# Who issues the transposing DMAs of the gathered rows: the sync engine instead of ScalarE

## What is computed

```python
logits = flat_x @ gate_w.T
scores = softmax(logits, axis=-1).T                 # 16 x T
topk_weight, topk_idx = top_k(scores, C)            # each expert takes C = 2 T / 16 = 1024 tokens
xg = flat_x[topk_idx]
g = einsum('ecd,eid->eci', xg, Wg)
u = einsum('ecd,eid->eci', xg, Wu)
h = gelu(g) * u
eo = einsum('eci,edi->ecd', h, Wd) * topk_weight[..., None]
flat_out = zeros.at[topk_idx].add(eo)
shared = gelu(x @ Sg.T) * (x @ Su.T) @ Sd.T         # for all tokens
x = x + layernorm(flat_out + shared)
```

## Time and profile before

| | us |
|---|---|
| median of three runs | 2062.1 (2060.92 to 2062.88) |
| the profiled execution, whole | 2058.04 |
| its span in the trace | 2056.0 |
| PE busy | 1999.6 (97%) |
| PEld busy | 1700.2 (83%) |
| DVE busy | 1360.3 (66%) |
| ACT busy | 1029.1 (50%) |
| POOL busy | 518.5 (25%) |

### The profile page before, as it was taken

How to read it: one execution, slowest core, us unless ns; L and a number is a source line. 1 busy time by engine, 2 the same in 40 slices (tenths; PEclk the granted TensorE clock), 3 DMA queues, 4 the chain that set the end, 5 groups by cost and what they waited for, 6 DMA issues and landing times.

```text
span 2056.0 us, 29853 instructions
## 1 busy us (share of the span) xinstructions
PE 1999.6 (97%) x11050; PEld 1700.2 (83%) x11050; DVE 1360.3 (66%) x2549; ACT 1029.1 (50%) x1900; POOL 518.5 (25%) x604
## 2 busy tenths in 40 slices
PE   7999999999999999999999999999999999998996
PEld 6888888888888888878887888888888888887885
DVE  6676576686666678676767666665656656565648
ACT  4564564574554434454445445454545455454445
POOL 0021021022021000224323332433243323331246
PEclk9999999999999999999999999999999999999998
DMA  3011111111115211234343334443444344435366
GB/s 116 1 42 43 62 63 42 61 62 42 42 55 205 84 62 48 97 96 84 84 98 89 94 81 102 81 111 79 109 86 101 80 108 92 97 86 154 76 216 164
DMA packets 118795, 179.67 MB, mean 87 GB/s; under 512 B 71952, under 2 KB 88464, under 8 KB 111504
## 3 DMA queue, kind: packets, MB, share of 16 engines
q1 hardware_dynamic: 30880, 124.55, 16.7%
q0 software_dynamic: 25392, 37.77, 11.6%
q10 hardware_dynamic: 62400, 15.73, 4.2%
HBM read 102.97 MB, written 59.31 MB: 79 GB/s over the span
## 4 chain that ended last, share of the span: by engine, by line
PE 62%; DVE 3%; ACT 2%; ACTq 2%; POOL 1%; issue 1%; DMA 0%; DVEq 0%; SPq 0%; POOLq 0%
PE mo_psD L1506 9%; PE mo_psG L60 7%; PE mo_psU L60 7%; PE mo_psU L62 7%; PE mo_psU L61 7%; PE mo_psG L62 7%; PE mo_psG L61 7%; PE mo_psD L1508 5%; ACTq L1592 2%; PE mo_psD L60 1%; PE mo_psD L62 1%; PE mo_psD L61 1%; PE mo_psX L1229 1%; ACT mo_halves L1586 1%; ACT mo_HF L1635 0%
## 5 line engine op out<-in xcount | busy, mean ns | idle before, releaser
L1635 ACT ACTIVATE mo_HF<-mo_psG 128x512 f32<-128x512 f32 x320 | 191.7, 599 | 410.7 <-PE mo_psU L62 376.8
L1506 PE MATMUL mo_psD<-wd,mo_H_hi 128*128 128x512 f32 x1024 | 364.6, 396 | 15.6 <-DVE OUT L1922 15.6
L2121 POOL DMA_INDIRECT ACC<-OUT,mo_GI x128 | 204.9, 1601 | 663.2 <-DVE OUT L1922 642.6
L1835 DVE TENSOR_TENSOR mo_HF<-mo_psU,mo_HF 128x512 f32<-128x512 f32 x320 | 220.4, 689 | 222.3 <-ACT mo_HF L1635 218.0
L1508 PE MATMUL mo_psD<-wd,mo_H_lo 128*128 128x256 f32 x1024 | 290.1, 283 | 0.0
L60 PE MATMUL mo_psG<-mo_XT_hi,wg_hi 128*128 128x512 f32 x640 | 256.1, 400 | 2.9 <-DVE mo_HF L1835 2.4
L60 PE MATMUL mo_psU<-mo_XT_hi,wu_hi 128*128 128x512 f32 x640 | 253.5, 396 | 0.0
L62 PE MATMUL mo_psU<-mo_XT_hi,wu_lo 128*128 128x512 f32 x640 | 252.6, 395 | 0.0
L62 PE MATMUL mo_psG<-mo_XT_hi,wg_lo 128*128 128x512 f32 x640 | 252.5, 395 | 0.0
L61 PE MATMUL mo_psU<-mo_XT_lo,wu_hi 128*128 128x512 f32 x640 | 252.4, 394 | 0.0
L61 PE MATMUL mo_psG<-mo_XT_lo,wg_hi 128*128 128x512 f32 x640 | 252.4, 394 | 0.0
(11 more groups left out here) (307 smaller groups left out, 4223.3 us busy)
## 6 DMA issues: line engine op xcount, KB each, us to landing
X1a<-wg_in SPq DMA_DIRECT2D x16, 1024.0 KB, 4.9
X1a<-wu_in SPq DMA_DIRECT2D x16, 1024.0 KB, 4.8
X1a<-wd_in SPq DMA_DIRECT2D x16, 1024.0 KB, 4.8
XN<-XG SPq DMA_DIRECT2D x8, 1088.0 KB, 4.1
X<-x_in SPq DMA_DIRECT2D x8, 1024.0 KB, 6.6
out_dram<-X SPq DMA_DIRECT2D x8, 1024.0 KB, 4.7
XN2T<-xn2T SPq DMA_DIRECT2D x8, 1024.0 KB, 4.0
mo_F<-ACC SPq DMA_DIRECT2D x7, 1024.0 KB, 12.0
```

Source lines behind the costliest of these rows:

```text
L1506: pe.matmul(psD[:, t % 2, :], h_hi, wd_both[:, it, :, :].rearrange("p z d -> p (z d)"), start=(it == 0), stop=False)
L1635: a.activation(HF[:, it % 2, :], psG[:, it % 2, :], ACT.Gelu).then_inc(s_gelu, 1)
L1835: v.tensor_tensor(HF[:, it % 2, :], psU[:, it % 2, :], HF[:, it % 2, :], ALU.mult).then_inc(s_mul, 1)
L2121: g.indirect_dma_start(out=io["ACC"], out_offset=bass.IndirectOffsetOnAxis(ap=GI[n % 2][:, 4 * tb + t:4 * tb + t + 1], axis=0), in_=OUT[:, ...
```

## The change

The function `turn_rows` moves from ScalarE's program to the sync engine's. ScalarE still splits the rows and increments s_half2, but issues no transposing DMA. The sync engine issues them in its loop over the experts: the one of half 1 of expert n between the loads of wg and wu of expert n + 1, the one of half 0 of expert n + 1 behind the load of wu, each behind a wait for s_half2. The first two expert blocks are left out as before.

```diff
@@ scalar
-            def turn_rows(b):
-                wait(a, s_half2, rows_index(b))
-                a.dma_start(out=turned[:, :, :].rearrange("p z (m t) -> p (z m) t", t=P),
-                            in_=halves[:, :, :, :, :].rearrange("p z k t d -> p (z k t d)"), transpose=True).then_inc(s_tt, 16)
-
...
                     if it < 2 and E0 + BY_PE <= b + 1 < D0:
                         split_rows(b + 1, it)
-                        if it == 1:
-                            turn_rows(b + 1)
                     task = weight_task(b, it)
@@ sync
+            def turn_rows(n, tb):
+                if 2 * n + tb >= BY_PE:
+                    wait(sp, s_half2, 2 * n + tb + 1 - BY_PE)
+                    sp.dma_start(out=turned[:, :, :].rearrange("p z (m t) -> p (z m) t", t=P),
+                                 in_=halves[:, :, :, :, :].rearrange("p z k t d -> p (z k t d)"), transpose=True).then_inc(s_tt, 16)
+
             for n in range(E):
                 load_w("d", n)
                 if n < E - 1:
                     load_w("g", n + 1)
+                turn_rows(n, 1)
+                if n < E - 1:
                     load_w("u", n + 1)
+                    turn_rows(n + 1, 0)
                 if 1 <= n < GROUPS - 1:
                     topk.store(sp, n + 1)
```

## The result

The changed kernel is faster: 2043.99 us median (2041.67 to 2045.05, four runs) against 2061.51 of the kernel before, measured on the same chip. The ratio is 0.9914, with a 95% interval of 0.9897 to 0.9931, a gain of 17.5 us. Two further sets of runs, each with its own runs of the kernel before, gave 2038.31 against 2058.1 (ratio 0.9908, interval 0.9893 to 0.9923) and 2043.04 against 2062.49 (0.9904, 0.9889 to 0.9920): gains of 19.8 and 19.5 us. The forecast was 2040.9 (range 2036 to 2052), a gain of 21.2.

A forecast was written before the change was run, and what follows sets the result against it. The prediction took TensorE to bound the kernel, with short waits caused by 30 transposing DMA issues on ScalarE. Terms 1.20 + 7.83 + 3.98 + 8.19 = 21.2 us off 2062.1 gave 2040.9 us, range 2036 to 2052.

The forecast's parts named there:

- The bound and the mechanism: TensorE bounds the kernel; it waits where ScalarE's transposing DMA issue stands before the evacuation of psD; 64.4 us mostly hidden.
- The term of the early blocks: 12 blocks from 899.98 to 1326.25: 7.83 us over 12 clean blocks of 34.87 us, to be removed.
- the term of the later ones: 16 blocks from 1326.25 to 1866.71: 3.98 us over 16 clean blocks of 33.53 us, to be removed.
- the last block's 8.19: Block from 1866.71 to 1908.43: 8.19 us excess from the longest transposing DMA issue and the slow clock behind it.
- Spare time of 0.3 us at the tightest place: Where mo_lo and a weight quarter both precede the evacuation: chain moves up about 1.8 us, a stall costs 1.57.
- The partial rival: VectorE's product and split still hold the evacuation, so only part is gained: 2044 to 2052 us, chance 0.11.
- The sync engine's queue: 30 issues added to an almost idle queue, costed at nothing; cover 19.2 us before the load of wd.
- The landing: Transposed rows reach VectorE's copies (L1750) in time: 4.3 us median, 12.3 at most, against 14.36; price zero.
- the slower rival: Transposing DMAs land too late for VectorE's copies at L1750, deciding from 14.4 us landing on; chance 0.04.
- The 8.18 us: Longest issue, the last transposing DMA on ScalarE's queue, placed where the burst of loads was in flight on the other queue.
- More than I count: More of the same stall in the last block in unprofiled runs: gain up to 25 us, 2034 to 2037, chance 0.08.
- no change: Stalls are displaced, coming from DMA traffic and not from the issue: about 2062 us, chance 0.07.

The follow-up runs named there:

- the second pair of profiles: The changed kernel and the kernel before, both unaltered, each profiled once more: spans 2036.2 and 2057.4 us.
- the complement: Kernel before with 29 transposing DMAs moved to the sync engine, the last one still on ScalarE's queue: 2043.46 against 2062.49 us, ratio 0.9908.

## Why the prediction was right, and where not

**The bound and the mechanism** were right: of 64.4 us of issue time only what reached TensorE counted. The work put back on ScalarE brought the stalls back without a DMA issue there.

**The sum.** 21.2 us was the forecast; the blocks of the changed kernel gave 20.3, the medians 17.5, 19.8 and 19.5. The term of the early blocks, 7.83, was 7.27, since in this profile five of the twelve stay about 0.1 us above the clean block (in the second the twelve are 0.1 over in sum); the term of the later ones, 3.98, was 3.62; the last block's 8.19 was 8.17, and with it the clock. The forecast lies 3.1 us below the first median. Of that 0.9 is this. The rest is of the size of the scatter of the stretch before the first block, which differs by up to 5.4 us between profiles and which I had taken as fixed; that it is this scatter is not shown for the runs without a profile, and the profiled execution, late in that stretch, was the fastest of its four. That the second pair of profiles differs by just 21.2 us is partly luck: the last stall was 0.4 us longer there, which made up for most of what stays.

**Spare time of 0.3 us at the tightest place.** Measured 0.40. The partial rival falls with it: with the issue gone, no evacuation was late.

**The sync engine's queue** cost nothing, as forecast. Issue times there reached 3.60 us at most.

**The landing.** The bound of 12.3 us was the traced maximum, and 14.36 was taken for the limit. It isn't the tightest pair: the kernel before has 13.76 us from issue to reader in every second block, and the changed kernel has the same:

```profile
1350.85 1.97 ACTq L1592 DMA_TRANSPOSE mo_turned<-mo_halves  x1
...
1364.61 1.38 DVE L1750 COPY mo_XTF<-mo_turned 128x1024 uint16<-128x1024 uint16 x2
```

So the slower rival would have begun 0.6 us earlier than the prediction says, at 13.8 us; with landings of 4.3 nothing hung on it. The last DMA on ScalarE's queue behind the burst took 14.4 in one kernel, so the upper bound from one trace was too low; the changed kernel isn't touched by that, since its last DMA goes ahead of the burst.

**The 8.18 us.** The forecast took the whole term as one that goes with the move; it did. Where it put the long issue down to the burst alone, it was incomplete: the same DMA behind the same burst took 2.47 and 1.72 us from another place in the queue. The move of the other 29 would have been enough to be rid of nearly all of it.

**More than I count, no change:** neither. The Trainium skill's remark that another issuer only saves the sequencer's time, usually small (the same page, section "Issuing engines are not separate DMA queues"), holds here in its first half: what was saved is that time and the slow clock behind the longest stall. Its second half doesn't hold so well: the issue takes 1.82 us of a landing of 4.3 (medians). It was worth 0.9% because the evacuations stood behind it in ScalarE's program.

**A sign that I gave and that doesn't hold:** I wrote that the "issue" waits of ScalarE before OUT would be gone. The view of the changed kernel still has them:

```profile
ACT OUT L1691 <- issue: 63.0, 27, 2.3
```

There is no issue on ScalarE any more; these are evacuations between two tiles of TensorE, 2.3 us each, for which no releaser was recorded. The second profile of the same kernel has no such row and puts the time down to TensorE, 128 waits where the first had 101:

```profile
ACT OUT L1691 <- PE mo_psD L1508: 240.5, 128, 2.8
```

The row for wg_hi is gone. "issue" in this view means only that nothing visible was waited for.

## What to carry to other kernels

A DMA issue is an instruction of the engine that issues it. Where a compute engine has a short slack in front of something that the bottleneck waits for, move the issue to an idle queue, and price it by the distances between repeated blocks: they include the ends of the stall and the slow clock behind it, which the idle time doesn't. Before moving, look for the reader's deadline: the same move with the DMA 12 us later cost 50 us more than the kernel it started from.

Terms measured one at a time needn't add up. Try the complement as well.

## What the runs showed of the hardware

- The time for which a queue is held by issuing a transposing DMA of 0.5 MB depends on its place among those the queue has carried: on ScalarE's queue, which carried nothing else here, about 1.33, 1.95, 1.85 and 1.79 us in turn, in every profile with that queue in use, with two or three exceptions of 2.2 to 3.2 us in each. The pattern moves by one place when one DMA is taken away ahead of them.
- With 4 MB of loads in flight from the other queue the issue took 8.18 us as the 30th, 1.72 as the 29th and 2.47 as the first, and the landing up to 14.4 us instead of 4.3.
- TensorE's clock was granted at 0.50 (1.2 GHz) after it had stood still for 6 us, and this cost 2.1 us beyond the stall. In the changed kernel's first profile it was 0.50 from 851 to 853, after a standstill of 3.55 us. The window of a block of the kernel before with a stall of 1.31 us has 1.00:

```profile
934.85:971.29 36.44, 35.13 (x195) 28.93 (x194) 24.26 (x36) 16.90 (x30) 16.62 (x14) 1.00 0.41 89
```
